# Four-stage transformer stack on one core: the softmax and squared-attention row sums taken from added-up probabilities instead of from one product per key block

## The reference

```python
# squared attention
attn = jnp.einsum('bqhd,bkhd->bhqk', q, k) ** 2          # q, k layer-normed per head
attn = jnp.where(mask, attn, 0.0)
o = jnp.einsum('bhqk,bkhd->bqhd', attn, v)
z = jnp.sum(attn, axis=-1)
o = o / (jnp.swapaxes(z, 1, 2)[..., None] + EPS)
return o.reshape(b, t, H * D) @ Wo.T
# gated (twice): one shared key and value head per token, picked by argmax of a gate
att = jax.nn.softmax(jnp.where(causal, q @ k_shared / sqrt(hd), -inf)); y = att @ v_shared
# mqa (between the gated ones): one key and value head for 16 query heads
attn = jax.nn.softmax(scores, axis=-1); ctx = attn @ v; out = ctx @ out_w.T + out_b
```

## Time and profile before

| | |
|---|---|
| runs of the kernel | 4794.02, 4797.77, 4806.56 us (median 4797.77) |
| the profiled execution | 4810.55 us; its span in the trace 4808.8 us |
| TensorE busy | 4292.6 us (89%) |
| VectorE, ScalarE, GpSimd busy | 1770.6 (37%), 1546.9 (32%), 847.3 us (18%) |
| mean granted TensorE clock | 0.961 of full speed |
| first act, second act | about 0 to 1200 us, 1200 to 4809 us of the span |

### The profile page before, as it was taken

How to read it: one execution, slowest core, us unless ns; L and a number is a source line. 1 busy time by engine, 2 the same in 40 slices (tenths; PEclk the granted TensorE clock), 3 DMA queues, 4 the chain that set the end, 5 groups by cost and what they waited for, 6 DMA issues and landing times.

```text
span 4808.8 us, 76616 instructions
## 1 busy us (share of the span) xinstructions
PE 4292.6 (89%) x32674; PEld 1781.0 (37%) x32674; DVE 1770.6 (37%) x2666; ACT 1546.9 (32%) x1985; POOL 847.3 (18%) x1495
## 2 busy tenths in 40 slices
PE   6899999996999898898898989989899897988987
PEld 4343434333333333333333333333333333333333
DVE  1222212122544444434444443443443444444342
ACT  1433333340223323323333333332222233232333
POOL 1311212121101211202112221211112012011012
PEclk8999999998999999999999999999999999999999
DMA  1001010003000100101001010000001001010010
GB/s 62 18 1 36 18 36 18 18 18 102 18 1 1 54 1 23 32 1 38 16 23 32 12 43 1 25 30 26 28 1 46 9 1 54 1 37 17 1 36 27
DMA packets 63405, 115.67 MB, mean 24 GB/s; under 512 B 8672, under 2 KB 9184, under 8 KB 63072
## 3 DMA queue, kind: packets, MB, share of 16 engines
q1 hardware_dynamic: 63072, 110.77, 7.2%
HBM read 77.19 MB, written 33.55 MB: 23 GB/s over the span
## 4 chain that ended last, share of the span: by engine, by line
PE 58%; DVE 6%; issue 5%; ACT 3%; DMA 2%; POOL 2%; POOLq 0%; SPq 0%; DVEq 0%; ACTq 0%
PE banks L1085 14%; PE banks L1043 10%; PE banks L995 9%; PE banks L1027 8%; PE banks L988 7%; DVE maxima_soft L811 5%; PE banks L1024 3%; ACT probs_soft L732 3%; PE banks L1052 2%; PE banks L1184 2%; DMA tiles_soft<-out 1%; PE banks L1159 1%; PE banks L1094 1%; POOL tiles_soft L637 0%; POOL rest_soft L705 0%
## 5 line engine op out<-in xcount | busy, mean ns | idle before, releaser
L811 DVE TENSOR_REDUCE maxima_soft<-banks 128x2 f32<-128x1024 f32 (+3 forms) x1152 | 1036.6, 953 | 1309.8 <-PE banks L1052 828.6
L732 ACT ACTIVATE probs_soft<-banks 128x1024 f32<-128x1024 f32 (+1 forms) x960 | 848.5, 936 | 1252.4 <-PE banks L1027 1250.2
L1043 PE MATMUL banks<-k_soft,q_soft 32*128 32x512 f32 (+3 forms) x4608 | 547.0, 544 | 69.6 <-ACT probs_soft L732 67.6
L646 POOL TENSOR_SCALAR_AFFINE_SELECT probs_soft<-probs_soft 128x512 f32<-128x512 f32 x384 | 239.2, 635 | 1963.5 <-ACT probs_soft L732 1961.8
L1027 PE MATMUL banks<-q_soft,k_soft 32*128 32x512 f32 (+3 forms) x4608 | 487.1, 505 | 0.0
L1085 PE MATMUL banks<-probs_soft,v_soft 128*32 128x512 f32 (+3 forms) x4608 | 435.6, 497 | 13.4 <-ACT shift_soft L718 9.5
L1085 PE MATMUL banks<-probs_soft,ones 128*32 128x512 f32 (+3 forms) x4608 | 433.5, 495 | 0.0
L732 ACT ACTIVATE probs_squared<-banks 128x1024 f32<-128x1024 f32 (+1 forms) x320 | 282.8, 936 | 387.7 <-PE banks L1027 387.6
L1043 PEld LDWEIGHTS banks<-k_soft,q_soft 32*128 32x128 f32 x4608 | 187.1, 186 | 320.1 <-issue 302.3
L1024 PE MATMUL banks<-shift_soft,ones 32*128 32x512 bf16 (+3 forms) x2304 | 202.3, 339 | 113.9 <-DVE maxima_soft L811 100.9
L995 PE MATMUL banks<-g_wv,xnT_soft 128*128 128x512 f32 x512 | 251.4, 625 | 27.4 <-DVE inverse_soft L917 21.2
(11 more groups left out here) (151 smaller groups left out, 4218.7 us busy)
## 6 DMA issues: line engine op xcount, KB each, us to landing
tiles_soft<-out SPq DMA_DIRECT2D x96, 256.0 KB, 2.9
rest_soft<-out SPq DMA_DIRECT2D x96, 256.0 KB, 3.0
out<-rest_soft SPq DMA_DIRECT2D x96, 256.0 KB, 2.0
tiles_squared<-in_x SPq DMA_DIRECT2D x32, 256.0 KB, 2.9
rest_squared<-in_x SPq DMA_DIRECT2D x32, 256.0 KB, 2.9
out<-rest_squared SPq DMA_DIRECT2D x32, 256.0 KB, 2.0
raw_wq<-in_squared_wq SPq DMA_DIRECT2D x1, 1024.0 KB, 6.2
raw_wk<-in_squared_wk SPq DMA_DIRECT2D x1, 1024.0 KB, 8.5
```

Of the source, the lines that this page charges most:

```text
L646: ins = pool.affine_select(out=cells, in_=cells, compare_op=ALU.is_ge, fill=0.0, base=0, pattern=[[0, HG], [1, P]], channel_multiplier=-1)
L732: act.activation(slot(ph, n)[:, 2 * a:2 * a + 2, 0:width], score_pair(e, a)[:, :, 0:width], ACT.Exp if soft else ACT.Square, scale=SCALE). ...
L811: ins = dve.reduce_max(m["maxima"][:, ph % 2, 2 * a:2 * a + 2, t, p], score_pair(e, a)[:, :, col:col + P * blocks], AX_X)
L1043: ins = pe.matmul(psum[:, score_bank(e, i), col:col + P * blocks], m["q"][D * i:D * i + D, ph % NG, P * t:P * t + P], k_of(ph)[D * i:D * i ...
```

## The change

TensorE no longer multiplies every probability block with ones. The blocks are first added up, element by element, in a new buffer `added` with one plane [128 x 4 heads x 512 queries] for each query chunk, and one product of that plane with ones gives the sums (`sm` now has two parts, chunk 0 and chunk 1, instead of A, B, C). GpSimd adds the whole blocks of chunk 1 (bursts 3 to 7: four additions of 128 x 2048). VectorE adds the blocks of the diagonal (bursts 0 to 2 for chunk 0; 8 and 9 for chunk 1, after GpSimd's last addition). `SLOTS` goes from 6 to 5, and a slot is free when both `av` and the additions that read it are through. In squared phases the key's scale moves into the Square: ScalarE takes it as a per-partition scale, which needs one instruction for each head and block; GpSimd makes it with a power (variance x 32 to the -1/2), and the scaling of the values is gone.

```diff
-SLOTS = 6
+SLOTS = 5
+ADDS = {1: [(384, 128, 384)], 2: [(0, 256, 256)], 4: [], 5: [(0, 512, 0)], 6: [(0, 512, 0)], 7: [(0, 512, 0)],
+        8: [(0, 384, 128), (384, 128, 384)], 9: [(0, 256, 256)]}
+WHOLE = (4, 5, 6, 7)
+CUT = (1, 2, 8, 9)
+SUMS_AT = (12, 6)
-WEIGHT = {"keys": 1.3, "rows": 1.2, "av": 3.2, "sm": 3.2, "q": 3.5, "q2": 3.5, "k2": 3.5, "kvar": 0.9, "v2": 3.5,
+WEIGHT = {"keys": 1.3, "rows": 1.2, "av": 3.2, "sm": 1.1, "q": 3.5, "q2": 3.5, "k2": 3.5, "kvar": 0.9, "v2": 3.5,
...
-HALVED = ("av", "sm", "q", "q2", "k2", "v2", "ks", "kall", "vall")
+HALVED = ("av", "q", "q2", "k2", "v2", "ks", "kall", "vall")
...
@@ phase
+    for n in ADDS:
+        if n < NKB - 1:
+            at[2 * n + 3].append(("add", ph, n))
+    if ph:
+        at[1].append(("add", ph - 1, NKB - 1))
...
-        at[h + 2].append(("more", ("sm", of, part)))
-        at[h + 3].append(("sm", of, part))
...
+    for c in range(NC):
+        of = ph - c
...
+        at[SUMS_AT[c]].append(("sm", of, c))
+        for event, later in sums_done(kinds[of // NG], of, c):
+            at[SUMS_AT[c] + later].append(event)
...
@@ wait_slot
-            wait_work(eng, ("sm", old[0], KEY_BURSTS[old[1]][1]))
+            wait_work(eng, ("av", old[0], KEY_BURSTS[old[1]][1]))
+            if old[1] in WHOLE + (3,):
+                eng.wait_ge(sg.whole_added, len(WHOLE) * old[0] + ADD_AFTER[old[1]])
+            else:
+                eng.wait_ge(sg.cut_added, len(CUT) * old[0] + ADD_AFTER[old[1]])
...
@@ GpSimd
+                elif u == "add" and e[2] in WHOLE:
+                    _, ph, n = e
+                    pool.wait_ge(sg.probs_ready, 2 * (of_kind["keys", ph, n] + 1))
+                    total = m["added"][:, 1]
+                    if n == 4:
+                        if ph:
+                            wait_work(pool, ("sm", ph - 1, 1))
+                        pool.tensor_tensor(total, slot(ph, 3), slot(ph, 4), ALU.add).then_inc(sg.whole_added, 1)
+                    else:
+                        pool.wait_ge(sg.whole_added, len(WHOLE) * ph + ADD_AFTER[n] - 1)
+                        if n == 7:
+                            pool.wait_ge(sg.probs_masked, masks_until(ph, "C", n))
+                        pool.tensor_tensor(total, total, slot(ph, n), ALU.add).then_inc(sg.whole_added, 1)
...
-                elif u == "vscale":
...
+                elif u == "kvar":
...
+                    pool.tensor_tensor(m["key_scale"][:, ph % NG, TPC * c:TPC * c + TPC, :].rearrange("p t i -> p (t i)"),
+                                       m["key_var"][:, c].rearrange("p t i -> p (t i)"), k["minus_half"][:], ALU.pow)\
+                        .then_inc(sg.key_scales, 1)
...
@@ ScalarE, squared stages
+                            for kb, _, cols, col in parts:
+                                for x in range(2):
+                                    i = 2 * a + x
+                                    ins = act.activation(slot(ph, n)[:, i, col:col + cols], score_pair(e, a)[:, x, col:col + cols],
+                                                         ACT.Square, scale=m["key_scale"][:, ph % NG, kb, i:i + 1])
...
@@ VectorE
+                elif u == "add" and e[2] in CUT:
+                    _, ph, n = e
+                    c, part, parts = KEY_BURSTS[n]
+                    dve.wait_ge(sg.probs_masked, masks_until(ph, part, n))
+                    total = m["added"][:, c]
+                    if n == 1:
+                        if ph:
+                            wait_work(dve, ("sm", ph - 1, c))
+                        dve.tensor_copy(total[:, :, 0:P], slot(ph, 0)[:, :, 0:P])
+                        ins = dve.tensor_tensor(total[:, :, P:CHUNK], slot(ph, 0)[:, :, P:CHUNK], slot(ph, 1)[:, :, 0:CHUNK - P], ALU.add)
+                    else:
+                        if n == 8:
+                            dve.wait_ge(sg.whole_added, len(WHOLE) * (ph + 1))
+                        dve.wait_ge(sg.cut_added, len(CUT) * ph + ADD_AFTER[n] - 1)
+                    for x, (col, width, q0) in enumerate(ADDS[n]):
+                        if x or n == 1:
+                            then(ins)
+                        sums = total[:, :, q0:q0 + width]
+                        ins = dve.tensor_tensor(sums, sums, slot(ph, n)[:, :, col:col + width], ALU.add)
+                    ins.then_inc(sg.cut_added, 1)
...
@@ TensorE
+                elif u == "sm":
+                    _, ph, c = e
+                    out = free(e)
+                    if not soft:
+                        pe.wait_ge(sg.query_squares, place["qsq", ph, c] + 1)
+                        pe.matmul(out, k["head_eps"][:].rearrange("p i d -> p (i d)"), m["query_square"][:, c], start=True, stop=True)
+                    pe.wait_ge(sg.cut_added, len(CUT) * ph + (2 if c == 0 else 4))
+                    for i in range(HG):
+                        ins = pe.matmul(out[D * i:D * i + D, :], k["ones"][:], m["added"][:, c, i, :], start=soft, stop=True,
+                                        skip_group_check=not soft)
+                    ready(e, ins)
```

105 lines of the change are left out of this document (48 added, 57 removed).

## The result

The changed kernel is slower: 4891.78 us in the median (4887.55 to 4899.13, 4 runs) beside 4798.87 for the kernel before, a ratio of 1.0195 (95% interval 1.0181 to 1.0209), or 93 us more. I had predicted 4641 us, in a range of 4480 to 4790. The profiled execution took 4888.94 us, its span 4887.2.

A forecast was written before the change was run, and what follows sets the result against it. TensorE, 89% busy, was taken as the bound, with a floor of about 2.5 us per half. Of 432 us removed 299 arrive, less 107, 32 and 3 of waits: 157 us, so 4641 us in the median, range 4480 to 4790.

The forecast's parts named there:

- What is removed: TensorE's products with ones: 6.85 us less in each of 48 soft phases, 6.45 in each of 16 squared, 432 us.
- How much arrives: Of the 432 us removed from TensorE, 299 shorten the time: 8, 94 and 104 in soft phases, 93 in squared.
- The floor: TensorE's bursts go round three bank pairs, so a half takes about 2.5 us however little TensorE work it holds.
- What the additions last: GpSimd's whole additions take 4.6 us each, 18.4 a phase; VectorE's 0.69, 1.23 and 1.77, together 8.1 with the copy.
- The added waits: Waits behind the additions: 107 us in soft phases, 32 in squared ones, 3 at the program's two ends.
- The turn: At a soft phase's end VectorE's burst 8 addition waits for GpSimd's last, delaying row reductions and evictions: 107 us in all.
- The key scale: In squared phases ScalarE's work grows from 18.7 to 27.8 us and GpSimd makes a power; both hide, nothing charged.
- Slots: A slot is asked for again ten halves after its burst, when `av` and addition are past; nothing charged.
- the turn rival: At the phase's turn GpSimd's chain slips, VectorE waits 6 to 8 us, evictions behind; at 7 a phase 4870; chance 0.11.
- The clock rival: More gaps on TensorE take another 0.02 off its granted clock, costing 86 us: near 4730; chance 0.10.
- The port rival: GpSimd and VectorE, both reading SBUF, hold each other up for whole instructions: 1 us a phase, 64 us, 4705; chance 0.08.
- Hidden waits: The additions' waits stay hidden on mostly idle GpSimd and VectorE, costing 20 to 40 us: near 4510; chance 0.20.

The follow-up runs named there:

- e1: The changed kernel with all additions left out on both engines, `added` filled once with ones: 4602.54 us, ratio 0.9586 to the kernel before.
- e13: The kernel before, with GpSimd adding only part B's blocks (three additions, one product with ones) in all 48 soft phases: 4695.74 us, ratio 0.9789.
- e11: The kernel before, with GpSimd adding only part B's blocks (three additions, one product with ones) in 18 of 48 soft phases: 4736.51 us, ratio 0.9872.
- e5: The changed kernel with bursts 8 and 9 added in the first chunk's plane, VectorE not waiting for GpSimd, and a second, 384-wide product: 4868.56 us, ratio 1.0134.
- e3: The changed kernel without VectorE's additions, GpSimd's kept: 4706.04 us, ratio 0.9796 to the kernel before.
- e2: The changed kernel without GpSimd's four whole additions, VectorE's kept and no longer waiting for GpSimd: 4717.87 us, ratio 0.9826 to the kernel before.
- e16: The changed kernel with each of GpSimd's additions one half later in the order, uncut: 5084.17 us, ratio 1.0593 to the kernel before.
- B everywhere: The kernel before, with GpSimd adding only part B's blocks in all 48 soft and 16 squared phases, ScalarE applying the key scale: 4660.87 us, ratio 0.9713.

## Why the prediction was wrong, point by point

*What is removed* (432 us): right, 411.

*How much arrives* (299): failed; 199 arrived, with the key scale's 19 paid from it. The floor was the right mechanism, and the failed step is how far I let it reach: I kept it for six unfilled phases and priced the other soft ones at 4.1 us (the middle of two ends) and 5.5 (0.8 of what is removed), for all three parts alike. In the profiled execution of e1 the eight shortest soft phases, 53.2 to 57.2 us long before, gained 1.1 us each, where I had 1.3 for the unfilled ones, and the other 40 gained 3.7 each, where I had 4.7 over 42. In e13, with part B's additions paid, the same eight gained 1.3: it was B that paid, as the 0.9 of 1.3 had said. The first act gained 59 us (its end is the first soft phase's start, 1250.0 and 1191.3) where I had 93. The 18 soft phases picked for e11 (picked by their gain, so the figure flatters) gained 128 us of 123 removed; the other 30 gained 27 of 206. What was missing turned into waits for maxima and probabilities, 137 us more than before, some 100 of them in those 40 longer phases.

*What the additions last*: right. GpSimd's took 4.52 for 4.6, VectorE's 0.69, 1.24 and 1.75 undisturbed for 0.69, 1.23 and 1.77 (burst 8's took 2.07 in the mean, beside GpSimd's masks); the copy took 0.43.

*The added waits* (142 in all): failed; 289, or 303 beside the old sums. The turn exists as described (6.25 us of VectorE's wait in phase 5, 1.74 on TensorE), and by e5 it is worth 23 to some 65 us, not 107. What was missing is the rest. GpSimd's additions alone cost 104 without any turn, through norms, masks and key squares behind 4.5 us in one queue: from e1 to e3 TensorE's wait for the soft tiles goes from 142 to 167 us, for masks from 11 to 46, for the key squares from 27 to 38, together the 72 us more that it idles. I had written that GpSimd stays under half its time and looked no further at who stands behind it. VectorE's alone cost 115. I had seen it delay row reductions, and evictions at the turn. But TensorE's wait for the maxima is the same in e1 and e2 (167 and 169 us); it is the rest of VectorE's queue that TensorE waits for, the scaled outputs (23 us more) and the gate's logits (15) first.

*The key scale* (0): 19 us, of which the profiled executions show 8 in the first act. I had let the power range up to 16 times 0.549 and found cover for it; it took 2.98 us. Which of the moved pieces costs the 19 was not parted.

*Slots* (0): nothing in the traces speaks against it; in the kernel after ScalarE's probabilities wait for an addition once, for 1.3 us. Six slots with these additions in place of the old sums weren't run.

*The rivals*: the turn rival named the right side and the wrong price; 4870 was its time. The wait that it named is there (235 us over 43 times, up to 8.9), but by e5 it costs 23 to some 65 us and not 7 a phase, so that the time came out near is luck. What a chain that slips further would do is shown by e16, at 5084. The clock rival (86 us) was true beside the others: 49 us with the removal, 69 more with the additions, and the mark that I had set (under 0.94) was passed at 0.921. The port rival (64) was true too; its share lies within the 70 us that the two engines' additions cost more together than apart, and within VectorE's 115, and was not measured alone. A step that failed is also one of form: I held clock, port and turn as cases that exclude each other, with 0.10, 0.08 and 0.11, though all three follow from the same edit and add up. Hidden waits, at 0.20, had nothing for it: even with free additions the time was 4603 and not 4510.

*The marks*: busy 3860 was forecast and 3999 measured, the difference being mostly the clock; idle 790 against 888; VectorE 47% against 46%, GpSimd 42% against 46%. The unfilled phases did not lose more than I had said: the eight shortest are 1.8 us longer each, for 2.1 (3.4 less 1.3). The mark on the clock was the one that was passed.

## What to carry to other kernels

Before removing work from a busy engine, split it by place and price each piece by its own stretch: here three cheap additions brought 137 us, and the rest of the same edit lost 231. An addition on an idle engine is priced by what stands behind it in its queue: GpSimd's 256, of 4.5 us each, cost 104 us by themselves, with the engine busy less than half of the time. Where the additions made many gaps on TensorE, its clock fell too (69 us beside 222 of idle time, from e1 to after), so waits and clock belong in one sum; but not every gap does that, for B everywhere has 44 us more idle time than the kernel before and 23 less for the clock. When several harmful mechanisms come from one edit, add them; don't share out the chances among them.

## What the runs showed of the hardware

A VectorE addition with both inputs in SBUF and a GpSimd instruction hold each other up: a 128x16 GpSimd subtraction took 1.55 us beside an addition of 1.75, against 0.23 alone. A VectorE copy of 1536 elements in SBUF took 5.25 beside GpSimd's additions, against 0.96 clear of them; one of 512 kept its 0.42 beside GpSimd's short casts. VectorE's reductions from PSUM stretched nothing (228 ns in e13). GpSimd's power took 2.98 us for 16 elements a partition and 0.55 for one. A VectorE copy of 512 elements in SBUF took 0.43 us, an addition of as many 0.69.
